# Attention kernel: the products with V of a head issued in two bursts instead of three

## What is computed

```python
Q = (X @ Wq.T + bq).reshape(B, S, H, d_head) * scale
K = (X @ Wk.T + bk).reshape(B, S, H, d_head) * scale
V = (X @ Wv.T + bv).reshape(B, S, H, d_head)
scores = jnp.einsum('bqhd,bkhd->bhqk', Q, K)
scores = jnp.where(causal[None, None], scores, -jnp.inf)
attn = jax.nn.softmax(scores.astype(jnp.float32), axis=-1).astype(X.dtype)
out = jnp.einsum('bhqk,bkhd->bqhd', attn, V).reshape(B, S, D)
return out @ Wo.T + bo
```

## Time and profile before

| | us |
|---|---|
| median of 3 runs | 2651.09 (2649.43 to 2652.48) |
| profiled execution, its own time | 2650.09 |
| span from its first to its last instruction | 2648.4 |
| PE busy | 2365.0 (89% of the span) |
| DVE busy | 2069.6 (78%) |
| ACT busy | 1169.7 (44%) |

### The profile page before, as it was taken

One profiled execution on the slowest core, in us unless ns is written; L12 is line 12 of the kernel. 1 busy time (PEld: TensorE's weight loads), 2 busy tenths in 40 slices (PEclk: granted clock), 3 DMA queues, 4 the chain that ended last, 5 costly groups with the idle time before them and its releaser, 6 DMA issues. The chain is left out here.

```text
span 2648.4 us, 41294 instructions
## 1 busy us (share of the span) xinstructions
PE 2365.0 (89%) x14084; PEld 1847.5 (70%) x14084; DVE 2069.6 (78%) x3420; ACT 1169.7 (44%) x2311; POOL 1157.6 (44%) x1249
## 2 busy tenths in 40 slices
PE   4994999999999999999999994399999997599993
PEld 2784788888888888888888873288888886343432
DVE  4875888888888888888888886577777776777765
ACT  1331555555555555555555552022222223266661
POOL 3442565665656656566565552145455441000000
PEclk9996899999999999999999997599999998699996
DMA  2002000000000000000000001000000001222214
GB/s 86 1 13 98 3 3 30 3 3 31 3 31 3 3 31 3 30 3 3 31 3 3 3 3 64 24 24 20 27 27 27 20 20 44 95 69 78 75 66 133
DMA packets 74320, 81.68 MB, mean 31 GB/s; under 512 B 21504, under 2 KB 57696, under 8 KB 72864
## 3 DMA queue, kind: packets, MB, share of 16 engines
q1 hardware_dynamic: 72096, 74.72, 8.7%
q10 hardware_dynamic: 2048, 4.72, 0.5%
HBM read 59.42 MB, written 19.79 MB: 30 GB/s over the span
## 5 line engine op out<-in xcount | busy, mean ns | idle before, releaser
L1043 DVE SCALAR_TENSOR_TENSOR mix_cv<-mix_pp,mix_cw,mix_cv 128x384 f32<-128x384 f32 (+4 forms) x864 | 493.0, 571 | 25.3 <-ACT mix_cv L966 4.5
L890 PEld LDWEIGHTS mix_pyd<-mix_xdt,mix_lm 128*128 128x128 f32 x2048 | 249.1, 193 | 56.7 <-issue 53.1
L966 ACT ACTIVATE mix_cv<-mix_pp,mix_cb,mix_cw 128x384 f32<-128x384 f32 (+1 forms) x288 | 182.1, 632 | 211.5 <-PE mix_pp L77 211.5
L75 PE MATMUL mix_pp<-l0in_XH,mix_wx_lo 128*128 128x384 f32 (+2 forms) x576 | 238.5, 414 | 39.3 <-DVE mix_ss L1032 23.3
L829 POOL TENSOR_TENSOR mix_xdt<-mix_xtok,l_dt 128x512 f32<-128x512 f32 x128 | 133.5, 1043 | 279.2 <-ACT mix_xtok L993 279.2
L1202 POOL TENSOR_TENSOR ffn_hl<-ffn_h,ffn_hh 128x512 fp32r<-128x512 f32 x112 | 144.3, 1288 | 250.5 <-ACT ffn_hh L1260 250.5
L941 PE MATMUL mix_pgt<-mix_wo,mix_gt 128*128 128x256 f32 x1024 | 244.9, 382 | 2.9 <-issue 2.2
L890 PE MATMUL mix_pyd<-mix_xdt,mix_lm 128*128 128x64 f32 x2048 | 244.4, 273 | 2.5 <-DVE mix_lm L1093 2.5
L822 POOL TENSOR_TENSOR mix_t<-mix_t,mix_xd 128x512 f32<-128x512 f32 x112 | 144.4, 1289 | 219.5 <-DVE mix_t L1057 136.9
L1725 DVE TENSOR_REDUCE att_tops<-att_psc 128x1 f32<-128x512 f32 (+3 forms) x384 | 190.0, 550 | 55.5 <-PE att_psc L1673 32.4
L941 PEld LDWEIGHTS mix_pgt<-mix_wo,mix_gt 128*128 128x128 f32 x1024 | 184.1, 190 | 31.2 <-issue 9.2
(11 more groups left out here) (337 smaller groups left out, 6677.4 us busy)
## 6 DMA issues: line engine op xcount, KB each, us to landing
mix_w_raw<-in_w_in SPq DMA_DIRECT2D x8, 1280.0 KB, 5.6
a_part<-att_sums SPq DMA_DIRECT2D x32, 256.0 KB, 5.1
ffn_raw<-in_wgu SPq DMA_DIRECT2D x56, 128.0 KB, 2.2
mix_ll<-cs SPq DMA_DIRECT2D x384, 4.0 KB
mix_wo_raw<-in_w_out SPq DMA_DIRECT2D x8, 512.0 KB, 6.5
ffn_draw<-in_wd SPq DMA_DIRECT2D x28, 128.0 KB, 2.1
q<-qkv_part SPq DMA_DIRECT2D x24, 128.0 KB, 1.9
k<-qkv_part SPq DMA_DIRECT2D x24, 128.0 KB, 1.9
```

Of the source, the lines that this page charges most:

```text
L75: pe.matmul(out, l_lo, r_hi, start=start, stop=False)
L890: last = pe.matmul(pyd[:, h * HP:(h + 1) * HP], lm[p % 2][:, h, :], xdt[p % 2][:, h * HP:(h + 1) * HP], start=True, stop=True)
L966: act.activation(conv_tile(k), pp[k % 2][:, halo:cols], ACT.Identity, bias=cb[:, it // 2, ct:ct + 1], scale=cw[:, it // 2, ct, 3:4]).then_ ...
L1043: last = dve.scalar_tensor_tensor(out, of, cw[:, g, ct, 3 - d:4 - d], out, ALU.mult, ALU.add)
```

## The change

Round one moves from k = 2 to k = 3, round two from k = 4 to k = 3. Rounds three and four stay at k = 6.

```diff
     SHARES = ((0, (0, 1, 2, 3)), (1, (0, 1)), (1, (2, 3, 7)), (1, (4, 5, 6)))
-    ROUNDS = {2: (0,), 4: (1,), 6: (2, 3)}
+    ROUNDS = {3: (0, 1), 6: (2, 3)}
```

## The result

| | before | after |
|---|---|---|
| median of 5 runs, us | 2650.98 (2648.52 to 2652.48) | 2665.13 (2664.17 to 2667.70) |
| ratio of the runs | | 1.0057 (95% interval 1.0043 to 1.0072) |
| span of the profiled execution, us | 2648.4 | 2663.4 |
| copy of the last head's `po`, start, us | 2589.9 | 2605.6 |

The kernel became slower, by 14 us between the medians and by 0.57%, or 15 us, as the ratio of the runs, where 15.3 us were forecast. The attention grew by 15.7 us in the profiled executions (last line of the table); the span grew by 15.0, because the stage behind the attention took 57.8 us there instead of 58.5.

A forecast was written before the change was run, and what follows sets the result against it. PE, 94% busy, was taken as the bound. 28 steps at 0.46 us (12.9) plus 2.4 us in three steps without scores made 15.3 us on 2650.09, 2665.4; the median, 1.0 above, was forecast at 2666.4 us, range 2657 to 2671.

The forecast's parts named there:

- row 3 (waits for exp 1): PE, ahead of the joint burst: row 3 could start at 6.72 us but waits for exp 1 until 6.81.
- joint burst starts: PE at k = 3: after row 3 ends at 7.15 us and 0.08 way in, the burst starts at 7.23.
- joint burst to s4a: PE at k = 3: rounds one and two joined take 0.98 + 0.97 - 0.10 = 1.85 us, the way out paid once.
- s5a later than before: PE behind the turn: s5a starts at 10.25 us against 9.79, so each of 28 steps costs 0.46, 12.9 us.
- The lap: PE's ring of three banks: product, reduction, bank free, next product take 1.17 us; s5a waits 0.31 us for s4a's bank.
- both rivals: In the experiments: only the number of ways in and out counts (0.18 us a pair), or a long burst starves DVE and ACT.
- Nothing gives it back: Behind s5a: neither DVE's 0.34 us idle nor the 0.33 wait ahead of row 2 absorbs the 0.46 us delay.
- The steps without scores: Steps 32 to 34: row 6 waits for exp 4 and starts 0.81 us late; three such steps cost 2.4 us.
- The saved way in and out: Rival, PE: a burst less saves 0.18 us in each of 32 heads, 5.8 us, giving 2645.3 us; chance 0.04.
- The lap didn't hide: Rival, PE at s5a: the ring doesn't hold s5a, only 0.15 us late; 6.6 us in all, 2657.7 us; chance 0.08.
- the granted clock: Rival, PE: one step in ten falls to 1.2 GHz, about 8 us more, 2674 us; chance 0.06.
- a head's loads stay hidden: SP's loads: they go out a step ahead of use, so they stay hidden and add nothing.

The follow-up runs named there:

- e2: Kernel before with round two alone moved, from k = 4 to k = 3, round one staying at k = 2; 2667.1 us, ratio 1.0063.
- e4: Changed kernel with the two pieces of query tile 4 swapped, s4b ahead of s4a; 2657.9 us, ratio 1.0027 to the kernel before.
- e9: e3 with round one's two waits moved from behind the turn to the start of k = 3; 2651.9 us, ratio 1.0004 to the kernel before.
- e6: Kernel before with round one alone moved, from k = 2 to k = 1, round two staying at k = 4; 2643.0 us, ratio 0.9974.
- e3: Kernel before with rounds one and two joined at k = 4, behind the turn; 2655.0 us, ratio 1.0016.

## Why the prediction was right

It held, and each place that it gave in a step came out within 0.02 us. The places, counted from the start of row 2's last product, and the distances, in us:

| | forecast | measured |
|---|---|---|
| s3 (waits for s0) | 0.14 | 0.15 |
| row 3 (waits for exp 1) | 0.52 | 0.53 |
| joint burst starts | 0.94 | 0.96 |
| joint burst to s4a | 1.85 | 1.84 |
| s4a to s5a | 1.17 | 1.18 |
| s5a later than before | 0.46 | 0.48 |

**The lap** carried the forecast, and e2, e4 and the 56 waits show it apart from both rivals. The last line follows from s5a: 2456.92 - 2452.94 = 3.98 after row 2's last product, against 2449.79 - 2446.29 = 3.50 before. Over 28 steps that is 13.4 us, for 12.9.

**Nothing gives it back:** row 2 still waits 0.33 us for exp 0, and 0.34 us of DVE's idle time stand unchanged ahead of s7a's reduction. Both moved along with s7a, as argued.

**The steps without scores:** row 2's last product in step 33 of the kernel before:

```profile
2575.69 0.27 PE L1687 MATMUL att_pst<-att_qs,att_ks 99*128 99x256 bf16 x1
```

Row 6 starts 3.94 us after it in the kernel after (2589.75 to 2593.69), and 3.11 before (2575.69 to 2578.80): 0.83, for 0.81. Three of them and the 13.4 make 15.9, beside the 15.7 us by which the last copy of `po` moved.

**The rivals.** The saved way in and out (chance 0.04) was not there to be saved: the turn pays it alone in the timeline after. The Trainium skill (TensorEngine Tiling (Array Packing), Key Properties) has it that a change of tiling mode drains the engine; the trace agrees once the changes are counted, three pairs in a step before and three after. Where e9 has one pair less, the step is no shorter, for other waits take its place. The lap didn't hide (chance 0.08), and the granted clock stayed at 1.00, the level of 2.4 GHz, over all 28 steps, with PE busy 8.49 of 9.24 us in the step shown. The busy time of one step, as in the earlier trace rows:

```profile
2452.66:2461.90 9.24, 8.49 (x66) 3.68 (x66) 6.69 (x17) 5.41 (x11) 0.00 (x0) 1.00 0.20 71
```

Two places of the prediction have more to them than it says. The wait ahead of s5a shows as 0.24 us, where 0.31 were forecast, though s5a is as late as forecast: the profile counts idle time from the modelled end of the turn, 0.23 us behind its start, and e4 shows that PE can go on after 0.16. And that a head's loads stay hidden because they go out a step ahead was right here and nearly not: the lead is 9.05 us in nearly all steps after the change, and loads of e6 took up to 8.90.

## What to carry to other kernels

Long independent work on an engine that fills a short ring of banks is also the cover for the ring's round trip: before merging or moving it, write down for every item which reduction frees its bank, and see whether the time between the two on the filling engine is still a whole lap. Count mode changes from the order of instructions after the edit, not by the number of bursts: a small product left behind may pay the change alone. And put such work where the engine waits today, then look at once for the next bound, which here was a load that until then had come just in time.

## What the runs showed of the hardware that was not expected

Two semaphore waits that had long been met cost PE 0.11 us in 25 of 28 steps of e3, where they stood right behind the turn (0.12 us from turn to burst, 0.01 with the waits moved ahead in e9). In the other three the burst followed after 0.01; why is not shown. In the kernel before the same two waits stand behind row 2's products and don't show: the burst starts 0.21 us after the last of them, of which 0.12 are that product's and 0.08 the way in the earlier trace rows. And the loads of Q and K took 8.9 us from first issue to first use in a late step of e6, though the DMA engines were busy only 23% of the time over all of e6's steps.
